# A depthwise convolution as four 128x32 column tiles, with each step's order and the PSUM pairs assigned anew

## The reference, cut to what matters

```
x = x + conv_block(group_norm(x))
  # depthwise 3x3 + bias, batch norm, relu, channels whose maximum < 4.0 set to zero,
  # pointwise 128x128, batch norm, relu, prune
t = tokens(x)                      # 784 tokens an image
t = t + spiking_attention(ln(t))   # q, k, v >= threshold; mask = causal and score > 0.1; mask @ v
t = t + moe(ln(t))                 # router, top 2 of 8 experts, 128 -> 512 -> 128, exact gelu
```

## Time and profile before

| what | value |
|---|---|
| median of 3 runs (lowest, highest) | 814.93 us (813.05, 819.28) |
| profiled execution, its device time | 816.78 us |
| its span, first to last instruction | 815.0 us |
| mean granted TensorE clock | 0.946 |
| busy in the span: TensorE, VectorE, ScalarE, GpSimd | 701.6, 592.2, 469.8, 503.1 us |

### The profile page before, as it was taken

The page is one execution under the profiler, slowest core; times in us unless marked ns, Lnnn a source line. Parts: engine busy times, 40 slices in busy tenths (PEclk is TensorE's granted clock), DMA queues, the critical chain, the costliest instruction groups (busy, mean ns, idle before and its releaser), DMA issues.

```text
span 815.0 us, 20024 instructions
## 1 busy us (share of the span) xinstructions
PE 701.6 (86%) x6460; PEld 547.8 (67%) x6460; DVE 592.2 (73%) x1804; ACT 469.8 (58%) x922; POOL 503.1 (62%) x501
## 2 busy tenths in 40 slices
PE   0579989999999999979966999999699999999633
PEld 0345656666666666655653988989699999999522
DVE  2758698888888877877755777796466666666867
ACT  0245475655566655546543978867477777777100
POOL 5100037776667777666676467777777777777740
PEclk9999999999999999999966999999899999999855
DMA  7701122331223233212213634454454554545998
GB/s 232 159 7 35 41 66 95 100 95 37 92 94 94 94 99 97 57 41 73 75 61 69 98 78 88 95 95 94 107 122 99 96 95 102 91 98 146 289 350 289
DMA packets 123037, 86.52 MB, mean 106 GB/s; under 512 B 96483, under 2 KB 105191, under 8 KB 122946
## 3 DMA queue, kind: packets, MB, share of 16 engines
q1 hardware_dynamic: 106034, 52.86, 27.3%
q0 software_dynamic: 13888, 26.03, 11.7%
q10 hardware_dynamic: 3024, 6.43, 2.3%
HBM read 30.50 MB, written 35.48 MB: 81 GB/s over the span
## 4 chain that ended last, share of the span: by engine, by line
PE 60%; DVE 16%; POOL 7%; DMA 6%; issue 5%; ACT 5%; DVEq 0%; SPq 0%; POOLq 0%; ACTq 0%
PE pair_a L562 16%; PE pair_d L768 12%; PE pair_b L751 5%; PE pair_c L751 5%; POOL expert_rows L514 4%; DMA out<-seen_g 4%; PE pair_c L593 3%; DVE p_area L1136 3%; ACT seen_g L870 2%; PE pair_d L662 2%; PE pair_c L648 2%; PE pair_b L582 2%; DVE xb_x L1373 2%; PE pair_d L633 2%; POOL dispatched_rows L504 2%
## 5 line engine op out<-in xcount | busy, mean ns | idle before, releaser
L504 POOL DMA_INDIRECT dispatched_rows<-p_area,pos x224 | 216.0, 964 | 97.8 <-issue 66.3
L514 POOL DMA_INDIRECT expert_rows<-conv_y,dest x210 | 224.0, 1067 | 75.1 <-issue 60.6
L768 PE MATMUL pair_d<-w,xb_x 128*128 x2520 | 168.4, 220 | 0.0
L562 PE MATMUL pair_a<-conv_y,p_area 128*128 128x392 f16 x864 | 162.3, 334 | 0.0
L938 ACT ACTIVATE xb_x<-seen_g 128x512 f16<-128x512 f32 x210 | 121.0, 626 | 60.2 <-PE pair_d L768 59.4
L768 PEld LDWEIGHTS pair_d<-w,xb_x 128*128 128x128 f16 x2520 | 152.3, 98 | 2.7
L1373 DVE TENSOR_TENSOR xb_x<-seen_g,xb_x 128x512 f16<-128x512 f32 x210 | 135.7, 688 | 18.7 <-ACT xb_x L938 16.3
L562 PEld LDWEIGHTS pair_a<-conv_y,p_area 128*128 128x128 f16 x864 | 82.9, 99 | 57.4 <-issue 2.6
L1389 DVE TENSOR_TENSOR conv_y<-pair_d,share 128x256 f32<-128x256 f32 x105 | 44.5, 423 | 67.8 <-PE pair_d L768 66.5
L751 PE MATMUL pair_b<-xrt,w 128*128 128x256 f16 x636 | 79.3, 275 | 2.1 <-DMA xrt<-dispatched_rows 2.1
L486 POOL TENSOR_TENSOR conv_y<-conv_y 128x784 f16<-128x784 f32 x16 | 26.3, 1642 | 87.8 <-ACT conv_y L832 87.6
(11 more groups left out here) (230 smaller groups left out, 1114.4 us busy)
## 6 DMA issues: line engine op xcount, KB each, us to landing
xb_x<-in_x SPq DMA_DIRECT2D x32, 392.0 KB, 4.0
p_area<-expert_rows SPq DMA_DIRECT2D x12, 784.0 KB, 18.1
t_all<-p_area SPq DMA_DIRECT2D x16, 392.0 KB, 3.0
out<-seen_g ACTq DMA_DIRECT2D x16, 392.0 KB, 9.5
t_all<-in_L_ffn_W SPq DMA_DIRECT2D x16, 256.0 KB, 6.2
dispatched_rows<-p_area,pos POOLq DMA_INDIRECT x224
expert_rows<-conv_y,dest POOLq DMA_INDIRECT x210
w<-expert_rows SPq DMA_DIRECT2D x4, 784.0 KB, 15.7
```

The lines of the kernel that those rows point to most:

```text
L504: pool.indirect_dma_start(xs, bass.IndirectOffsetOnAxis(ap=pos[:, u, t, k:k + 1].bitcast(U32), axis=0), rows[:, u, t, :].bitcast(U32), Non ...
L514: pool.indirect_dma_start(ys, bass.IndirectOffsetOnAxis(ap=dest[:, place, slot, s:s + 1].bitcast(U32), axis=0), y[:, t % STORE_DEEP, s, :] ...
L562: last = T.matmul(pa[:, h * BANK:h * BANK + HALF], tap_diag[:, wp, tap, :], padx[:, xp, u, ky + 14 * h:ky + 14 * h + 14, kx:kx + SIDE], st ...
L768: last = T.matmul(dst, ghl[:, t % 2, gp, f * TILE + s * P:f * TILE + (s + 1) * P], w2[:, wp, bass.ds(w0 + f * P, P)], start=False, stop=(f ...
```

## The change

It replaces the 54 matmuls of an image's convolution by 72 that each use a quarter of the array's columns. For each tap and half there are four, one for each group of 32 channels. The contraction axis of 128 rows holds four copies of the 32 channels: planes (high, low, high, low) against weights (high, high, low, low), so that one matmul makes all products at once. It carries a `tile_position=(0, 32 g)`.

That layout needs the planes of a group stacked over the partitions. SyncE does it through DRAM: one DMA writes both planes of the image to `conv_planes`, and when it has landed, four DMAs load `stacked`. Convolution waits for the stack (`stacked_0`, `stacked_1`) and no longer for `xhi_ready` and `xlo_ready`. `make_taps` has 5 instructions where there were 19. The depthwise weights are loaded by four small DMAs where there was one.

The order in each step is new as well, and so are the PSUM pairs: the scores go to `pair_c`, the third tile to `pair_a` (before: `pair_d` and `pair_b` in turn); the group mean goes to `pair_a`, the weights' mean to `pair_b` (before: both `pair_c`).

```diff
+    planes = nc.dram_tensor("conv_planes", (2, 2, P, PLANE), F16, kind="Internal").ap()
...
-        padx = conv_y[:, 0:pad_words].bitcast(F16).rearrange("p (n u h w) -> p n u h w", n=2, u=2, h=PAD)
+        plane = conv_y[:, 0:PLANE].bitcast(F16).rearrange("p (n c) -> p n c", n=2)
+        padx = plane.rearrange("p n (h w) -> p n h w", h=PAD)
+        stacked = conv_y[:, PLANE:pad_words].bitcast(F16).rearrange("p (u g c) -> p u g c", u=2, g=PARTS)
...
+            def stack_planes(i, j, u):
+
+                if some(64 * j):
+                    gate(f"stacked_{u}", 64 * j)
+                if some(i - 1):
+                    gate("conv_ready", i - 1)
+                gate("xhi_ready", i + 1)
+                gate("xlo_ready", i + 1)
+                sp.dma_start(planes[u].rearrange("n c x -> c n x"), plane[:, :, :]).then_inc(S["plane_out"], 16)
+                gate("plane_out", 16 * i + 16)
+                for s in range(PARTS):
+                    sp.dma_start(stacked[s * GROUP_CHANNELS:(s + 1) * GROUP_CHANNELS, u, :, :],
+                                 planes[u, s % 2].rearrange("(g p) x -> p g x", p=GROUP_CHANNELS)).then_inc(S[f"stacked_{u}"], 16)
...
-                for p in range(first, end):
-                    tap, h = p // 2, p % 2
+                    if step.image(3):
+                        gate("seen_ready", NT * (i - 2) + 3)
+                    gate("taps_ready", 1)
+                    gate(f"stacked_{u}", 64 * j + 64)
+                for tap in range(first, end):
                     ky, kx = tap // 3, tap % 3
-                    for m, (wp, xp) in enumerate(((0, 0), (0, 1), (1, 0))):
-                        last = T.matmul(pa[:, h * BANK:h * BANK + HALF], tap_diag[:, wp, tap, :],
-                                        padx[:, xp, u, ky + 14 * h:ky + 14 * h + 14, kx:kx + SIDE],
-                                        start=(tap == 0 and m == 0), stop=(tap == TAPS - 1 and m == 2))
+                    for h in range(2):
+                        for g in range(PARTS):
+                            last = T.matmul(pa[g * GROUP_CHANNELS:(g + 1) * GROUP_CHANNELS, h * BANK:h * BANK + HALF], tap_w[:, g, tap, :],
+                                            stacked_rows[:, u, g, ky + 14 * h:ky + 14 * h + 14, kx:kx + SIDE],
+                                            start=(tap == 0), stop=(tap == TAPS - 1), tile_position=(0, g * GROUP_CHANNELS))
...
-                    if t == 1:
-                        pe.wait_ge(S["sv_ready"], i + 1)
-                    if t >= 2:
-                        pe.wait_ge(S["seen_ready"], i * NT + t - 1)
-                    pair = (pd, pb)[t % 2]
+                    if t in (1, 3):
+                        pe.wait_ge(S["seen_ready"], i * NT + (t + 1) // 2)
+                    if t >= 4:
+                        pe.wait_ge(S["seen_ready"], i * NT + t)
...
                 if att:
-                    see(att[0])
-                if with_weights(step):
-                    high_weights(step.k - WEIGHTS_FROM)
+                    see(att[0], range(5))
                 if step.normed():
                     deviations(step)
+                if att:
+                    see(att[0], (5, 6))
```

More of the change, by code:

```diff
@@ L344, in body @@
                         sp.dma_start(x1[:, u, :], x_img[bass.ds(i + 2, 1)].rearrange("a c l -> c (a l)")).then_inc(S[f"again_{u}"], 16)
+                if step.image(0):
+                    i, j, u = step.image(0)
+                    stack_planes(i, j, u)
                 if step.image(0) and (not isinstance(step.k, int) or step.k + 2 < IMAGES):
@@ L439, in _ @@
             const(G.memset(avg_all[:], 1.0 / P))
-            const(G.memset(padx[:], 0.0))
+            const(G.memset(plane[:, :, :], 0.0))
             const(G.memset(two_rows[:], 1.0))
@@ L547, in weight_mean @@
                 pe.wait_ge(S["stage_loaded"], 32 * E)
-                T.matmul(pc[:, BANK:2 * BANK], avg_all[:], staged[:, 0, n, :], start=True, stop=True).then_inc(S["w_mean"], 1)
-            def conv(i, u, first, end):
+                if some(n):
+                    pe.wait_ge(S["w_hi_ready"], 2 * n)
+                if some(n - 1):
+                    pe.wait_ge(S["sv_ready"], n - 1)
+                T.matmul(pb[:, 0:BANK], avg_all[:], staged[:, 0, n, :], start=True, stop=True).then_inc(S["w_mean"], 1)
@@ L566, in conv @@
+                if end == TAPS:
                     last.then_inc(S["conv_ready"], 1)
@@ L615, in values, with scores @@
                 last.then_inc(S["v_ready"], 1)
-            def scores(i, ts):
+            def scores(step, i, ts):
                 for t in ts:
@@ L710, in body @@
                 if cnv:
-                    conv(cnv[0], cnv[2], 14, 18)
+                    conv(step, *cnv, 7, 9)
                 if add:
-                    queries(step, add[0])
+                    queries(add[0])
                     values(add[0])
                     keys(add[0])
+                if moe:
+                    rank(moe[0], pd)
                 if cnv:
                     pointwise(cnv[0])
-                if moe:
-                    rank(moe[0], pd)
             steps(pe, body)
@@ L861, in copy_xt, with see @@
                              ACT.Copy).then_inc(S["xt_ready"], 1)
-            def see(i):
-                for t in range(NT):
+            def see(i, ts):
+                for t in ts:
                     if t == 0:
@@ L913, in body @@
                     high_rows(*moe)
+                if with_weights(step):
+                    high_weights(step.k - WEIGHTS_FROM)
                 if cnv:
@@ L1031, in make_taps @@
                 link = Chain("dve_taps", 0)
-                link(V.tensor_scalar(dw64[:, :], dw_w[:, :], WSCALE, None, ALU.mult))
-                for tap in range(TAPS):
-                    last = V.tensor_scalar(tap_diag[:, 0, tap, :], ident[:], dw64[:, tap:tap + 1], None, ALU.mult)
-                link(last)
-                for tap in range(TAPS):
-                    last = V.scalar_tensor_tensor(out=tap_diag[:, 1, tap, :], in0=ident[:], scalar=dw64[:, tap:tap + 1],
-                                                  in1=tap_diag[:, 0, tap, :], op0=ALU.mult, op1=ALU.subtract)
-                last.then_inc(S["taps_ready"], 1)
+                half = PARTS // 2 * GROUP_CHANNELS
+                V.tensor_reduce(same[:, :], ident[:, :].rearrange("p (s c) -> p c s", s=PARTS), AX.X, ALU.add)
+                link(V.tensor_scalar(dw64[:, :, :], dw_w[:, :, :], WSCALE, None, ALU.mult))
+                link(V.tensor_copy(dw16[:, :, :], dw64[:, :, :]))
+                link(V.tensor_tensor(dw64[half:P, :, :], dw64[half:P, :, :], dw16[half:P, :, :], ALU.subtract))
+                V.tensor_tensor(tap_w[:, :, :, :].rearrange("p g t c -> p (g t) c"), bc_mid(same[:, :], PARTS * TAPS),
+                                bc_last(dw64[:, :, :].rearrange("p g t -> p (g t)"), GROUP_CHANNELS), ALU.mult).then_inc(S["taps_ready"], 1)
             def group_sums(part, image):
@@ L1250, in body @@
                     spikes(sv[:, :], pb[0:TT, 0:NT * P], add[0], V_THRESH, "v_ready", "sv_ready")
-                    spikes(sk[:, :], pc[:, 0:L], add[0], K_THRESH, "k_ready", "sk_ready")
                 if moe:
                     place(z_link, moe[0], moe[2], pd)
+                if add:
+                    spikes(sk[:, :], pc[:, 0:L], add[0], K_THRESH, "k_ready", "sk_ready")
+                if with_weights(step):
+                    low_weights(step.k - WEIGHTS_FROM)
                 if cnv:
```

172 lines of the change are left out of this document (94 added, 78 removed).

## The result

The changed kernel takes **837.7 us** in the median of 4 runs (834.9 to 843.0); the kernel before took 815.8 us beside it. The ratio is **1.026, 95% interval 1.022 to 1.030: slower**. The profiled execution took 842.96 us, span 841.1. Three later chips gave every kernel about 250 us more, the kernel before too (1062.8, 1076.4 and 1062.8 us), with stops of some 12 us in most steps; results from them are marked "stopping chip", and are compared only with others from the same one.

What follows compares the result with a forecast made beforehand. TensorE was taken to set the pace before, and the ring of 21.8 us a step after. Start, step 8 and tail losses against shorter steps summed to -16 from 816.8, 800.8; median forecast 799 us, range 784 to 826.

Steps and rivals of the forecast that it cites:

- TensorE, 18.9 us, "no longer the pace": TensorE's busy time a step: 13.3 other work, 4.0 convolution, 1.6 layout changes; sum 18.9 us, so not the pace.
- VectorE, "its instructions are the same": VectorE's step: same instructions but for step 0, 20.2 us without its waits, 21.9 with weights.
- single delay of 5: One delay of 5 us, left out of the 23.45 us taken for each of eight steps before the change.
- Rival 4: An unfound wait takes the place of TensorE's, so the time stays within 1%; chance 0.06.
- The ring, 21.8 us a step: Loop from positions through sends, low plane, stack and convolution back to positions: 43.6 us over two steps, pace 21.8.
- p: Time from the low plane's end to a full stack through DRAM: 9.4 us, with ends 7.3 and 15.5.
- The three steps with weights, 22.2: Three steps with weights fall from 24.04 to 22.2 us each: VectorE's 21.9 and a little unhidden; -5.5 in all.
- Step 8, +6: SyncE's image load waits for the low weights, so the planes and step 9's convolution come late: +6 us, once.
- Start, +4.5: The first image's planes wait in SyncE's full DMA queue; first convolution from 42.3, costing +4.5 us.
- the -2 in each of three steps: The three steps up to the mark of 128.52, 24.3 us each before, get 2 us shorter each.
- Rivals 1 and 2: Rival 1: stack late, pace 24.9, 840 us, chance 0.15. Rival 2: tiles not fully overlapping, 847 or 873 us, 0.11.

Runs made afterwards that it cites:

- a_fix_fill: Changed kernel with both GpSimd subtractions on VectorE, step 8's low-weights wait moved behind image load and stack, eight unread matmuls added a step: 799.6 us, ratio 0.981.
- a_dvesub: Changed kernel with GpSimd's two subtractions a step given to VectorE: 826.4 us, ratio 1.015 to the kernel before.
- after_again: The changed kernel itself, unaltered, run again beside later experiments on one chip: 834.5 us, from two executions.

## Why the prediction was wrong

The range of 784 to 826 missed the time by 12 us, and the forecast had the sign wrong. By its own steps:

- **TensorE, 18.9 us, "no longer the pace":** in size right at full clock (18.2 busy in the step of 22.09 above; 19.05 in a_fix_fill's, which has 1.3 us added). The tiles took 0.0475 us, in the bounds. But the step took the clock of 1.00 for given, compared the busy time with a whole step, and put TensorE off the path; here it failed. TensorE lay on the path all the same, for 9.0 us of the changed kernel's step of 25.54 and 8.9 of a_dvesub's of 24.12: VectorE's key spikes, scores, convolution, last Sign, VectorE. The prediction has no sum for this path, and the lower clock lengthens it. Undone last, the clock is worth 19.8 us, the largest of the three costs.
- **VectorE, "its instructions are the same":** this step failed too. The instructions are the same and their durations are not, since the order beside them moved: 9.8 us of excess became 32 to 39. The trace of before had the sign of it, one instruction of 4.14 us among twins of 0.29 (the line below), in the "single delay of 5" that I set aside as chance. Rival 4, "a wait that I did not find", was this, at 0.06 and within 1%.

```profile
350.52 4.14 DVE L1122 TENSOR_SCALAR pw_masked<-w_t,gs 128x128 f32<-128x128 f32 x1
```

- **The ring, 21.8 us a step:** not the pace of the changed kernel's profiled loop steps, though close beneath it. p was near its size, 10.1 in the step above and 9.5 to 11.0 in the other loop steps and steps with weights, where 9.4 was foreseen, and a DMA released the convolution in three steps only (18.8 us in all; in five steps of after_again). With GpSimd's work shortened the steps took 20.7 to 21.7 us, and in that of 20.71 the convolution waited 1.5 us for the stack, whose DMAs have 9.4 us of the chain of waits. Without collisions and at full clock the steps 9 to 14 of a_fix_fill took 21.9 us. That 21.9 matches 21.8 is luck: the chain of waits there is VectorE's, whose foreseen 20.2 with the 2.0 moved to it makes 22.2.
- **The three steps with weights, 22.2:** 25.9, and 23.7 without collisions and with the matmuls. There VectorE is busy 22.3 us a step and has the 2.0 us that were moved to it, so the 1.5 above the forecast need no other cause.
- **Step 8, +6:** the mechanism as told (the load of 227.69 behind a wait of 12.5, the convolution at 241.10 released by the stack); moving the wait gave 7.0. The step itself took 33.9 where about 28 was foreseen.
- **Start, +4.5:** the first convolution at 42.52 for 42.3; the stretch to mark 5 came 4.2 us later instead of 1.5 earlier, as the -2 in each of three steps didn't come.
- **Rivals 1 and 2** didn't happen in this kernel: the stack came in time but for three convolutions, and weight loads of a quarter's width stay hidden.

Put together, on chips with the kernel before at 815.8 to 816.2: 837.7 less 11.3 for the collisions (net of 2.0 us more work for VectorE a step), less 7.0 for step 8, less 19.8 for the clock, makes 799.6. The shares hold for this order of undoing: with the collisions left in, the eight matmuls gave nothing (837.4). Only the second of the three was in the prediction. Shown is each of these three by an undone cause. Not shown is why the old order keeps the clock and the new one doesn't. The share of idle time alone does not decide it: a step with 18.20 of 22.09 us busy ran at 1.00, and one with 24.68 of 26.95 at 0.87. Nor is it shown whether the eight matmuls could be fewer.

## What to carry to other kernels

A change of order leaves no duration as it was: for each instruction of VectorE with two SBUF inputs ask what GpSimd reads at that moment, before and after. And an engine with idle time isn't off the critical path: relieved TensorE idled, its clock fell, and the path ran through its slower matmuls. Follow the path that goes over two engines within one step before calling either of them free. Where a tuned kernel shows one instruction ten times as long as its twins, price it before moving its neighbours.

## What the runs showed of the hardware

- An elementwise product of 112x56 numbers, 0.20 us, took 3.51 beside two GpSimd subtractions of 1.64 and 1.83; in pieces of 0.42 and 0.55 us no VectorE instruction lost more than 0.38.
- GpSimd's memsets in place of the subtractions left three delays of VectorE, of 0.3 to 0.6 us; beside its indirect sends alone (0.94 us each) no VectorE instruction of the changed kernel's image stage lost over 0.2 us.
- The subtractions of 128x784 and 112x896, 1.64 and 1.82 us on GpSimd, are about 1 us of VectorE's time each: moved, they cost 2.0 of its time a step and gained 8 to 11 us in all.
- A weight load of 32 columns takes 0.107 us in the mean, one of 128 columns 0.098 to 0.099: a quarter of the columns saves nothing. The matmuls behind it follow at 0.0475 us in four tiles, so most of the loads run beside them.
- Work without use can pay: eight matmuls of 0.16 us a step took 20 to 21 us off a launch of 820, and the granted clock of the loop steps rose from 0.86 to 1.00.
